# One-hots built in both orientations on VectorE, lookups six visits ahead, and GpSimd waiting for landing after every fourth group, in a graph attention layer with a mixture of experts

## The reference

```python
def _L0_gnn_ref(h, W, a_src, a_dst, src, dst):
    N, DEG = (6250, 16)
    z = jnp.einsum('ni,hid->nhd', h, W)
    es = jnp.einsum('nhd,hd->nh', z, a_src)
    ed = jnp.einsum('nhd,hd->nh', z, a_dst)
    e = es[src] + ed[dst]
    e = jnp.where(e >= 0, e, SLOPE * e)
    m = jax.ops.segment_max(e, dst, num_segments=N)
    ex = jnp.exp(e - m[dst])
    denom = jax.ops.segment_sum(ex, dst, num_segments=N)
    alpha = ex / denom[dst]
    msg = alpha[:, :, None] * z[src]
    out = jax.ops.segment_sum(msg, dst, num_segments=N)
    return out.reshape(N, HEADS * OUT_DIM)
...
x = x + _L0_gnn_ref(_layernorm(x, axis=-1), L0_gnn_W, L0_gnn_a_src, L0_gnn_a_dst, src, dst)
x = x + _L0_ffn_ref(_layernorm(x, axis=-1)[None], ...)[0]
```

## Time and profile before

| what | us |
|---|---|
| median of 3 runs (lowest, highest) | 3249.27 (3246.93, 3252.94) |
| span of the profiled execution | 3732.8 |
| first stage, to the first gather | 0 to 126 |
| edge stage, first gather to last | 126 to 2949 |
| third stage | 2977 to 3093 |
| routing lists | 3093 to 3172 |
| experts | 3172 to 3640 |
| last stage | 3640 to 3733 |

### The profile page before, as it was taken

How to read it: one execution, slowest core, us unless ns; L and a number is a source line. 1 busy time by engine, 2 the same in 40 slices (tenths; PEclk the granted TensorE clock), 3 DMA queues, 4 the chain that set the end, 5 groups by cost and what they waited for, 6 DMA issues and landing times. The chain is left out here.

```text
span 3732.8 us, 63946 instructions
## 1 busy us (share of the span) xinstructions
PE 2518.1 (67%) x12555; PEld 2103.9 (56%) x12556; DVE 1639.2 (44%) x4398; ACT 905.0 (24%) x2612; POOL 2073.2 (56%) x1912
## 2 busy tenths in 40 slices
PE   5385857667666677777757676667686663899960
PEld 3274746556555556556545565555565561799950
DVE  6352534435333444344424344444343588322239
ACT  2121212212111221112211121212121221455542
POOL 1466756666655755556655566655566333455543
PEclk9686867778777777778777777777776855999985
DMA  4233322232322322222222222322323120733347
GB/s 142 75 79 80 84 77 75 76 79 73 79 76 70 85 68 74 75 77 76 76 78 66 75 76 75 83 73 75 79 74 80 47 69 8 247 114 100 105 123 213
DMA packets 227739, 322.62 MB, mean 86 GB/s; under 512 B 95506, under 2 KB 165114, under 8 KB 227706
## 3 DMA queue, kind: packets, MB, share of 16 engines
q0 software_dynamic: 87744, 243.02, 23.7%
q1 hardware_dynamic: 119994, 62.90, 6.1%
q10 hardware_dynamic: 19968, 16.35, 1.7%
HBM read 287.77 MB, written 33.50 MB: 86 GB/s over the span
## 5 line engine op out<-in xcount | busy, mean ns | idle before, releaser
L529 POOL DMA_INDIRECT ring<-z_table,idx_ring x1612 | 1733.7, 1076 | 1095.0 <-DVE msg L618 610.7
L708 PE MATMUL psMb<-msg,S 128*128 128x260 f32 x3608 | 1162.0, 478 | 0.4 <-DVE msg L618 0.4
L688 PE MATMUL psTb<-ident,S 128*128 128x128 f32 x1804 | 361.7, 336 | 881.7 <-DVE S L583 704.7
L708 PEld LDWEIGHTS psMb<-msg,S 128*128 128x128 f32 x3608 | 815.8, 238 | 139.9 <-DVE msg L618 1.0
L688 PEld LDWEIGHTS psTb<-ident,S 128*128 128x128 f32 x1804 | 273.9, 175 | 1011.4 <-issue 739.4
L590 DVE TENSOR_TENSOR earg<-es_edge,psEb 128x16 f32<-128x16 f32 x451 | 77.3, 171 | 1615.8 <-remote 1052.7
L698 PEld LDWEIGHTS psEb<-nodes,ST 128*128 128x128 f32 x3608 | 558.3, 236 | 109.7 <-issue 107.6
L698 PE MATMUL psEb<-nodes,ST 128*128 x3608 | 578.7, 288 | 32.4 <-issue 31.4
L618 DVE TENSOR_TENSOR msg<-ring,msg 128x1024 f32<-128x1024 f32 x451 | 550.6, 1221 | 0.4 <-issue 0.2
L671 ACT ACTIVATE msg<-earg 128x16 f32<-128x16 f32 x451 | 97.2, 216 | 1281.6 <-DVE earg L608 848.8
L665 ACT COPY ST<-psTb 128x512 f32<-128x512 f32 x451 | 260.8, 578 | 519.8 <-remote 433.2
(11 more groups left out here) (200 smaller groups left out, 1579.4 us busy)
## 6 DMA issues: line engine op xcount, KB each, us to landing
ring<-z_table,idx_ring POOLq DMA_INDIRECT x1612
w_all<-in_L_ffn_w_dram SPq DMA_DIRECT2D x32, 512.0 KB
b_sb<-in_L_ffn_b_dram ACTq DMA_DIRECT2D x108, 128.0 KB
got<-pair_rows SPq DMA_DIRECT2D x48, 256.0 KB, 2.8
idx_ring<-src_idx SPq DMA_DIRECT2D x403, 2.0 KB
z_table<-z_out SPq DMA_DIRECT2D x49, 130.0 KB, 1.9
norm_rows<-xnc SPq DMA_DIRECT2D x49, 128.0 KB, 1.7
xs<-in_x_dram SPq DMA_DIRECT2D x4, 1536.0 KB, 20.2
```

Of the source, the lines that this page charges most:

```text
L529: nc.gpsimd.indirect_dma_start(ring[:, s, c, :], None, z_table, bass.IndirectOffsetOnAxis(ap=idx_ring[:, s, c:c + 1], axis=0)).then_inc(b_ ...
L688: last = nc.tensor.transpose(psT[s % 2][:, c * P:(c + 1) * P], S[:, s, c, :], ident[:, :])
L708: last = nc.tensor.matmul(psM[s % 2][:, 0:ROW], S[:, s, c, :], msg[:, s % 4, c, :], start=c == 0, stop=c == G - 1)
```

## The change

- The constants: MSG_TO_ACC is 4, and there are AHEAD = 6 (visits by which the lookup of ed runs ahead), PAUSE = 4 and ROWS = 4.
- The first stage computes the destinations modulo 128 as bfloat16 and stores them in DRAM (`dst_rows`).
- ScalarE issues for each visit a DMA that reads the 512 destinations of the group as one row and spreads it over all partitions (`load_dst`, into one of four slots `dst_bc`). VectorE compares it with the partition's number and has ST (`make_ST`). TensorE's `transpose` and ScalarE's `copy_ST` are gone. ST of a group's two visits is the same; what tells their tiles apart is S, built from `loc` as before, which has no one for an edge of the other tile.
- S and ST have eight slots each; they lie in the tiles 16 to 47 of `xs`. So those tiles of x are loaded again at the start of the third stage, and its additions wait for them.
- `msg` has eight slots, `psM` four banks; `psE` has four banks with two visits in each, and `e_add` waits for both visits of a bank (`both`).
- GpSimd waits after the fourth and the eighth slot of the ring until that group has landed.
- The semaphores of the first stage are cleared and freed, with a barrier over all engines; the five semaphores ending in `apart` are one.

```diff
-MSG_TO_ACC = 2
+MSG_TO_ACC = 4
+AHEAD = 6
+PAUSE = 4
+ROWS = 4
...
+    KEPT = NT - 1 - 32
...
+                sp.wait_ge(a_mod, 1)
+                sp.dma_start(dst_rows.rearrange("(b p f) -> p b f", p=P, f=P), dst_mod_h[:, :, :]).then_inc(a_mod_saved, 16)
...
+                        step(nc.vector.tensor_scalar(dst_mod[:, :, :], dst_raw[:, :, :], P - 1, None, ALU.bitwise_and))
+                        nc.vector.tensor_copy(dst_mod_h[:, :, :], dst_mod[:, :, :]).then_inc(a_mod, 1)
...
+        nc.clear_and_free_semaphores(nc.allocated_since(before_a))
+        nc.all_engine_barrier()
...
-            S = sb(ctx, "S", [P, SR, G, P])
-            ST = sb(ctx, "ST", [P, 2, G * P])
+            S = xs[:, KEPT:KEPT + 2 * SR, :].rearrange("p (s o) c -> p s (o c)", o=2).rearrange("p s (g e) -> p s g e", g=G)
+            ST = xs[:, KEPT + 2 * SR:KEPT + 4 * SR, :].rearrange("p (s o) c -> p s (o c)", o=2)
+            dst_bc = sb(ctx, "dst_bc", [P, ROWS, G * P], BF16)
...
+            msg = sb(ctx, "msg", [P, SR, G, ROW])
+            psE = [ps(ctx, f"psEb{i}") for i in range(SR // 2)]
+            psM = [ps(ctx, f"psMb{i}") for i in range(4)]
...
+                        if s % PAUSE == PAUSE - 1:
+                            pool.wait_ge(b_landed[s], 16 * G * (k * len(range(s, GROUPS, RING)) + r + 1))
...
+                    def make_ST(v, s, r):
+                        at, use = s % ROWS, r * (SR // ROWS) + s // ROWS
+                        dve.wait_ge(b_dst[at], 16 * (k * len(range(at, VISITS, ROWS)) + use + 1))
+                        if not early(v, SR):
+                            dve.wait_ge(b_dest, base + v - SR + 1)
+                        nc.vector.tensor_scalar(ST[:, s, :], dst_bc[:, at, :], iota_p[:, 0:1], None, ALU.is_equal).then_inc(b_ST, 1)
...
-                        dve.wait_ge(b_dest, base + v + 1)
+                        both = v + 2 - s % 2
+                        dve.wait_ge(b_dest, base + (min(both, VISITS) if isinstance(v, int) else both))
...
-                    pipeline(dve, VISITS, SR, SR, [(look_up, 3), (e_add, 2), (one_hot, 0), (e_lrelu, 2), (accumulate, 3 + MSG_TO_ACC),
-                                                   (e_shift, 2), (message, 3), (e_clamp, 2)])
+                    pipeline(dve, VISITS, SR, 2 * SR, [(look_up, AHEAD + 1), (e_add, AHEAD), (make_ST, 0), (e_lrelu, AHEAD),
+                                                       (accumulate, AHEAD + 1 + MSG_TO_ACC), (e_shift, AHEAD), (one_hot, AHEAD),
+                                                       (e_clamp, AHEAD), (message, AHEAD + 1)])
...
+                    def load_dst(v, s, r):
+
+                        group = act.value_load(visit_group[0:1, bass.ds(v, 1)], min_val=0, max_val=GROUPS - 1)
+                        if not early(v, ROWS):
+                            act.wait_ge(b_ST, base + v - ROWS + 1)
+                        act.dma_start(dst_bc[:, s % ROWS, :], over(dst_rows[bass.ds(group * (G * P), G * P)].unsqueeze(0), [P, G * P])
+                                      ).then_inc(b_dst[s % ROWS], 16)
...
-                    pipeline(act, VISITS, SR, 8, [(locate, 0), (copy_ST, 2), (open_group, 2), (exponent, 3)])
+                    pipeline(act, VISITS, SR, 2 * SR, [(load_dst, 0), (locate, AHEAD + 1), (open_group, AHEAD + 2), (exponent, AHEAD + 3)])
...
-                        if not early(v, 2):
-                            pe.wait_ge(b_arg, base + v - 1)
+                        if s % 2 == 0 and not early(v, SR):
+                            pe.wait_ge(b_arg, base + v - SR + 2)
...
-                        if not early(v, 2):
-                            pe.wait_ge(b_acc, base + v - 1)
+                        pe.wait_ge(b_S, base + v + 1)
+                        if not early(v, 4):
+                            pe.wait_ge(b_acc, base + v - 3)
...
-                    pipeline(pe, VISITS, SR, 5, [(transpose, 0), (destination, 1), (weigh, 3)])
+                    pipeline(pe, VISITS, SR, 2 * SR, [(destination, 0), (weigh, AHEAD + 1)])
...
+                for i, lo in enumerate((KEPT, 2 * PART, 3 * PART)):
+                    hi = (i + 2) * PART
+                    sp.dma_start(xs[:, lo:hi, :], x[lo * P:hi * P].rearrange("(t p) c -> p t c", p=P)).then_inc(c_x[i], 16)
```

More of the change, by code:

```diff
@@ L120, in sem @@
     def sem(name):
-        return whole.enter_context(nc.semaphore(name))
+        return nc.alloc_semaphore(name=name)
     def sb(ctx, name, shape, dt=F32):
@@ L722, in gnn_moe_kernel @@
         c_slot = sem("c_slot"); c_low = sem("c_low"); c_eq = sem("c_eq"); c_by_tile = sem("c_by_tile")
+        c_x = [sem(f"c_x{i}") for i in range(3)]
         c_by_part = sem("c_by_part"); c_listed = sem("c_listed")
```

78 lines of the change are left out of this document (39 added, 39 removed).

## The result

The changed kernel takes **3554.7 us** (median of 4 runs, 3552.09 to 3556.56), beside 3248.1 us for the kernel before in the same comparison (3244.62 to 3252.94): a ratio of 1.0953, 95% interval 1.0937 to 1.097. It is 9.5% slower. The forecast was 3080 us, 5% faster, with a range up to 3520; neither the sign nor the range held. The nearest of the cases was the first rival, at 3496 us.

What follows compares the result with a forecast made beforehand. The prediction took late TensorE completions during streaming gathers, which stop GpSimd, to bound the edge stage. Terms -602 + 60 + 52 + 304 + 10 = -176 us, carried to the runs' 3249, gave 3080 us; range 2990 to 3520.

Steps and rivals of the forecast that it cites:

- the first rival: Edge stage: the removed waits belong to the profile only, GpSimd already bounds the runs; 3496 us, slower; chance 0.26.
- the largest doubt: Whether the profile's excess over the runs lies in the removed waits or elsewhere, when carrying the saving to the runs.
- -176 us: Sum of all forecast terms against the profiled 3732.8 us, giving a changed profile of 3556 us.
- -602 + 60 us: GpSimd's waits for VectorE's message product vanish with lookups six visits ahead (-602 us); a tenth is left as residue (+60).
- the wait for landing: GpSimd's pause after each fourth group of gathers: 3.1 us times 98, +304 us, bounds 176 to 340.
- the 483.5 us: Profiled execution of the kernel before, 3732.8 us, less the median of its runs, 3249.3 us.
- 0.30 us per gather: Unexplained gap before each of 1612 gathers, offered as a possible place for the profile's excess over the runs.
- The compare: VectorE's added compare per visit, 221 us in all, stretches GpSimd's gathers by 0.24 us per us: +52 us, bounds 0 to 221.
- the second rival: VectorE's added compare blocks GpSimd's gathers outright, costing 221 instead of 52 us: 3249 us, no change; chance 0.10.
- Lookups ahead: Destination matmuls issued six visits early give late TensorE completions some 30 us of slack; GpSimd's message waits go, -602 us.
- Other edits: First-stage passes and store, boundary barrier, x tiles loaded again in the third stage: together +10 us, from 5 to 20.
- TensorE's clock: Edge stage: GpSimd's pauses may idle TensorE and keep it at 1.2 GHz, about 3480 us; chance 0.05.

## Why the prediction was wrong

**The base of the sum.** The step that failed is the one called "the largest doubt": to carry -176 us from the profiled 3732.8 to the runs' 3249, "as it stands" or "in proportion". Where GpSimd never stops, the -602 + 60 us do not exist. On the chips of the runs that term is 0: the kernel before has no wait for a message at all. Of the prediction's steps this one carries the sign. That the forecast of the profile's span, 3556 us, was met to 1 us is luck as well: it was worked out from a late chip and met on a quiet one, where the 60 us held back for late completions stood in for the 57 that the wait for landing had too little; what the changed kernel takes on a late chip is not known.

**What the 483.5 us were.** I offered two places for them: the recording's own waits, or 0.30 us per gather. The gap of 0.30 us is there on the quiet chips too (497.1 us in all), so the account by which my forecast held was false. The first rival put them into the waits, which is where they are, and blamed the recording; it is the chip or the occasion. It kept 119 us of waits in the runs (602 - 483.5), where there are none, because gathers on the quiet chip lose 1865.5 - 1733.7 = 132 us more to VectorE (another 28 us lie outside the stage). Its mechanism is right, a pause in a queue that is never empty; that its 3496 us comes so near is in part luck, since the 119 us that it gained too much and 120 us that it had the gathers lose too much (52 instead of -68) cancel. I took the gathers' busy time as fixed; it grows when the stops go.

**The wait for landing.** The mechanism was right, its size a little low. Landing took 2.05 us (2.1 by the working); what comes after it 1.90 us, not 0.45 + 0.84; and the two waits that I gave to the first filling are paid as well, 100 and not 98. That makes 3.65 x 100 = 365 us against +304, and 364.5 measured; even the upper bound, 340, was too low.

**The compare.** +52 us with bounds of 0 and 221, by a price per us of VectorE work. The size was too high and the form of the price was wrong: what a compare costs depends on how many gathers begin in it and how much of it is left then, 26 us in the changed kernel. My bound of nothing came from the clamp's unchanged 168 ns, but it is the gather that waits and not VectorE's operation. Along with the compare came an order of steps in which fewer gathers begin in a one-hot, so that in all the gathers lost 1865.5 - 1797.3 = 68 us rather than gaining 52, some of it by the pauses themselves. The Trainium skill ("SBUF — State Buffer", "Who interferes with whom") would have a VectorE scalar operation in a two-port mode block GpSimd. The traces agree with it for the gather that is hit (1515.62 above, and 144 of 145); no view names the mode. To take the whole 221 us from it, as the second rival did, was the error.

**Lookups ahead.** Where completions are late, the change does what the forecast says of them: "remote" waits fall from 1042.9 to 39.3 us. But the stops are only halved (113 to 56), and the kernel without the wait keeps 395 us where I had 60 left over, since ScalarE's instructions come slowly there. The forecast put ScalarE's part at nothing because it was busy for 554 us of 2823; on quiet chips that holds.

**Other edits.** From the last gather's end to the end of the program the quiet-chip traces have 3238.5 - 2479.6 = 758.9 us before and 3554.9 - 2779.2 = 775.7 after; with 5.4 us before the first gather (123.3 to 128.7) that is 22 us, against +10 and bounds of 5 to 20. The x tiles that are loaded again cost nothing in it: GpSimd's addition to them (L841) begins at 2812.48, 0.08 us after the step ahead of it. What makes up the 17 us behind the last gather stays open.

**The sum as it should have been**, on a quiet chip, from the kernel before at 3238.5: gaps +361 (857.9 - 497.1), gathers -68, the rest +22 or so: 3554.

TensorE's clock was no rival in the end: GpSimd bounds the stage in every quiet-chip trace, also in the changed kernel, where the mean granted clock of the whole span was 0.727.

## What to carry to other kernels

When a trace's span and the times of the runs differ by far more than the runs do among themselves, they don't describe the same execution, and a forecast from the one says nothing of the other until it is known what the difference is; work out both accounts, and let the one that matches the times carry the forecast. Ask of every wait that an edit adds whether the queue it goes into is ever empty: if that queue's busy time and its own short gaps fill the stage, the wait is paid in full, here 100 times 3.65 us. When one engine stretches another's instructions, look at when they start and end before you price it per us: here nearly all of the cost fell on gathers that began inside an operation of VectorE. And a change that cures a stall should be timed where the stall is and where it is not, since the same wait was worth between -0.9 and -1.8% in one place and +9.5% in the other.

## What the runs showed of the hardware

The same program took 3244 us on two chips and 3731 to 3830 on two others, at equal lengths of its matmuls and products. On the latter, while GpSimd issues gathers without a break, TensorE's completions reach VectorE late, so that it waits up to 33.4 us, and register instructions of ScalarE that take some 0.06 us elsewhere (L699) take up to 1.4 us: 15 to 25 instructions of over 0.65 us in the kernel before, 960 to 990 in the changed one without the wait. What in these chips or occasions does it was not found.

A gather takes 0.95 us alone. If it starts inside VectorE's product of 128x1024, its one-hot or its compare of 128x512, it ends 0.82 us after that operation. Nothing of the kind was seen for VectorE's operations on 16 columns or for `accumulate`, which reads PSUM: no gather of the kernel before that began in one of them ends so.
The same section of the Trainium skill's page "SBUF — State Buffer" infers that a VectorE operation on two SBUF tensors does not hold up the writing of descriptors by GpSimd, since it takes only the read side of the shared ports. The traces do not speak against that. The gather also reads its indices from SBUF, and it is held when the product or the one-hot runs at its start: in the trace of the changed kernel 106 gathers have such an operation begin after their own start and still running 0.83 us on, and 103 of them take 0.95 us as if alone. That the held part is the reading of the indices is my inference.
